# The gates of the final sum: made on all partitions by TensorE instead of loaded 128 times

## What is computed

```python
mod = (_silu(L0_c) @ L0_wmod).reshape(32, 6, 1, -1)
sa, ca, ga, sb, cb, gb = (mod[:, 0], ..., mod[:, 5])
gb = (2 * (gb >= 0) - 1) * jnp.maximum(jnp.abs(gb), 0.25)      # one row of 128 per sequence
...
x = x + gb * _L0_ffn_ref(h, ...)                               # x: (32, 256, 128)
```

## Time and profile before

| | us |
|---|---|
| three runs | 1588.82 (median), 1579.2, 2478.22 |
| profiled execution, its own time | 1589.78 |
| its span, first to last instruction | 1588.0 |
| of this, last stage (from SP's first row load) | 1536.1 to 1588.0 |
| busy: PE, DVE, ACT, POOL | 1366.6, 1180.9, 885.0, 868.0 |
| mean granted TensorE clock | 0.954 |

### The profile page before, as it was taken

The page is one execution under the profiler, slowest core; times in us unless marked ns, Lnnn a source line. Parts: engine busy times, 40 slices in busy tenths (PEclk is TensorE's granted clock), DMA queues, the critical chain, the costliest instruction groups (busy, mean ns, idle before and its releaser), DMA issues. The chain is left out here.

```text
span 1588.0 us, 42685 instructions
## 1 busy us (share of the span) xinstructions
PE 1366.6 (86%) x13344; PEld 1063.3 (67%) x13345; DVE 1180.9 (74%) x3082; ACT 885.0 (56%) x1918; POOL 868.0 (55%) x1279
## 2 busy tenths in 40 slices
PE   1499999999999999999999999962599999999950
PEld 1266777767777776777777676641588888888850
DVE  4567888888888888788888887866666666666647
ACT  1166777777777777777777777652133333333310
POOL 2045577677767767676776776663233333333334
PEclk9999999999999999999999999985799999999985
DMA  6433443444344354444434533300211111111139
GB/s 213 123 100 83 129 118 94 118 118 114 103 126 121 92 133 110 103 110 118 122 88 120 128 98 90 87 24 14 59 48 43 46 43 42 46 43 45 42 94 295
DMA packets 176591, 152.61 MB, mean 96 GB/s; under 512 B 21491, under 2 KB 159097, under 8 KB 176036
## 3 DMA queue, kind: packets, MB, share of 16 engines
q1 hardware_dynamic: 159096, 123.07, 30.1%
q0 software_dynamic: 8448, 16.93, 3.3%
q10 hardware_dynamic: 8880, 10.49, 1.9%
HBM read 89.37 MB, written 61.55 MB: 95 GB/s over the span
## 5 line engine op out<-in xcount | busy, mean ns | idle before, releaser
L988 ACT ACTIVATE probs<-p_exp 128x512 f32<-128x512 f32 x768 | 446.5, 603 | 183.6 <-PE p_exp L812 164.3
L1402 POOL TENSOR_SCALAR_AFFINE_SELECT probs<-probs 128x256 f32<-128x256 f32 (+1 forms) x768 | 365.4, 485 | 286.4 <-ACT probs L988 278.3
L1166 DVE TENSOR_REDUCE mx<-p_max 128x2 f32<-128x512 f32 x512 | 351.4, 687 | 169.9 <-PE p_max L786 168.9
L647 POOL DMA_INDIRECT pair_out<-on,v x136 | 133.6, 982 | 284.7 <-ACT on L557 279.3
L784 PE MATMUL p_max<-kt,qt 96*128 96x256 bf16 x1024 | 198.6, 275 | 40.5 <-DMA kt<-k_parts 19.7
L835 PE MATMUL p_out<-probs,v 128*32 128x256 f32 (+1 forms) x4096 | 221.0, 333 | 14.0 <-POOL probs L1402 7.5
L812 PE MATMUL p_exp<-qt,kt 100*128 100x256 bf16 x1024 | 196.7, 273 | 16.8 <-DMA qt<-max_parts 14.0
L621 DVE TENSOR_TENSOR ot<-ot,p_max 128x512 f32<-128x512 f32 x136 | 93.5, 688 | 125.8 <-PE p_max L508 106.5
L1169 DVE TENSOR_REDUCE mx<-p_max 128x4 f32<-128x512 f32 x256 | 173.2, 676 | 2.1 <-PE p_max L795 2.0
L835 PEld LDWEIGHTS p_out<-probs,v 128*32 128x32 f32 x4096 | 112.4, 109 | 85.4 <-POOL probs L1402 24.4
L1449 POOL DMA_INDIRECT rows_sorted<-h,idx x128 | 137.4, 1074 | 50.7 <-ACT probs L988 28.6
(11 more groups left out here) (169 smaller groups left out, 2757.9 us busy)
## 6 DMA issues: line engine op xcount, KB each, us to landing
qt<-q_parts SPq DMA_DIRECT2D x64, 384.0 KB
q_parts<-part_h SPq DMA_DIRECT2D x96, 128.0 KB, 2.0
kt<-k_parts SPq DMA_DIRECT2D x128, 96.0 KB
v<-rows_sorted SPq DMA_DIRECT2D x136, 65.0 KB, 1.8
q_parts<-part_m SPq DMA_DIRECT2D x64, 128.0 KB, 2.0
kt<-k_parts SPq DMA_DIRECT2D x128, 64.0 KB
qt<-pair_out SPq DMA_DIRECT2D x32, 256.0 KB, 5.4
mods<-mod_rows SPq DMA_DIRECT2D x32, 192.0 KB
```

The source lines that it names most:

```text
L647: nc.gpsimd.indirect_dma_start(pair_out, bass.IndirectOffsetOnAxis(rows_in[:, j.slot, DIM:DIM + 1].bitcast(U32), 0), rows_out[:, j.slot, : ...
L988: nc.scalar.activation(probs[:, g % 2, k, :], p_exp[:, k, :], ACT.Exp, scale=SCALE).then_inc(exp_done.sem, 1)
L1166: m = V.reduce_max(mx[:, w, 1, :, h8:h8 + 1].rearrange("p t o -> p (t o)"), p_max[:, bank, :].rearrange("p (t k) -> p t k", t=2), AX.X, ne ...
L1402: G.affine_select(out=blocks, in_=blocks, compare_op=ALU.is_ge, fill=zero, base=0, pattern=[[0, 2 if k < 2 else 4], [1, P]], channel_multi ...
```

## The change

The gate loads go. PE makes each group's gates on all partitions: a column of the identity, repeated 128 times as the stationary operand, times the 32 gate rows gives one sequence's row on every partition, so two matmuls fill 256 columns of a bank. Four banks serve as the four slots: the two of `p_exp` and the two of `p_max` whose expert products are over (PE waits for `hid_ready`). Before it fills a slot again, PE waits for the multiply four groups earlier (`fin_step`). DVE's multiply reads its gates from PSUM and waits for `gb_ps`, which PE raises once a group.

```diff
-        fin_gb = (pair_view[:, FIN_RING * NF:FIN_RING * (NF + GROUP * DIM)]
-                  .rearrange("p (a b c) -> p a b c", a=FIN_RING, b=GROUP))
+        fin_gb = (p_exp[:, 0, :], p_exp[:, 1, :], p_max[:, 0, :], p_max[:, 1, :])
...
-                sp.dma_start(fin_gb[:, g.slot, :, :],
-                             mod_rows[bass.ds(g.n * GROUP, GROUP), 3 * DIM:4 * DIM].unsqueeze(0)
-                             .to_broadcast([P, GROUP, DIM])).then_inc(fin_loaded[g.slot], 16)
...
             tiles(pe, body)
 
+            pe.wait_ge(hid_ready, FFN_TILES)
+            for g in range(NB // GROUP):
+                if g >= FIN_RING:
+                    pe.wait_ge(fin_step, 2 * (g - FIN_RING) + 2)
+                for j in range(GROUP):
+                    b = g * GROUP + j
+                    m = nc.tensor.matmul(fin_gb[g % FIN_RING][:, j * DIM:(j + 1) * DIM],
+                                         idf[0:NB, b:b + 1].to_broadcast([NB, P]), mrow[:, 3, :], start=True, stop=True)
+                m.then_inc(gb_ps, 1)
...
-                dve.wait_ge(fin_loaded[g.slot], 48 * (g.turn + 1))
+                dve.wait_ge(fin_loaded[g.slot], 32 * (g.turn + 1))
...
                 dve.wait_ge(fin_step, 2 * g.n + 1)
+                dve.wait_ge(gb_ps, g.n + 1)
                 fo = fin_out[:, g.slot, :].rearrange("p (b t c) -> p b t c", b=GROUP, c=DIM)
-                V.tensor_tensor(fo, fo, fin_gb[:, g.slot, :, :].unsqueeze(2).to_broadcast([P, GROUP, NT, DIM]), ALU.mult).then_inc(fin_step, 1)
+                gb = fin_gb[g.slot][:, 0:GROUP * DIM].rearrange("p (b c) -> p b c", b=GROUP)
+                V.tensor_tensor(fo, fo, gb.unsqueeze(2).to_broadcast([P, GROUP, NT, DIM]), ALU.mult).then_inc(fin_step, 1)
```

More of the change, by code:

```diff
@@ L313, in adaln_block @@
         fin_step = sem("fin_step")
+        gb_ps = sem("gb_ps")
         fin_done = sem("fin_done")
```

## The result

Over 20 runs each, the changed kernel takes 1578.97 us (median), the kernel before 1587.59 us (1588.82 in the three runs known ahead). The ratio is 0.9948, with an interval of 0.9933 to 0.9963: 5.9 to 10.6 us less, real, and well within 2%. One execution of each stands far outside (2478.22 us, and 2014.93 at a granted clock of 0.654) and is left out of the ratio. The forecast was 1582.6 us.

What follows compares the result with a forecast made beforehand. It took the last stage (52 us) to be paced mostly by DVE and POOL blocking each other. First POOL end 1542.65 + fifteen steps of 2.35 (35.25) + 2.96 + 1.78 gave 1582.6 us; range 1573 to 1590.

Steps and rivals of the forecast that it cites:

- Where the time lies: Only the last stage is at stake, from 1536.1 to 1588.0 us: 52 us or 3.3% of the span.
- The start: Last stage's first add waits for the second row load, not the gate load: gain 2.0 us, bounds 0 to 2.2.
- The new step: Time per group in the last stage, set between engines, DMAs and ring of four slots: 2.35 us.
- the late circle: DVE's add comes after POOL's start and waits for it, as before: 2.71 + 0.08 = 2.79 us a group.
- The mixture's share: Last stage: even mixture of groups with DVE's add after POOL's start (2.79) and before it (1.81): 2.30 us.
- The engines' lower bound: Last stage, DVE's add going before POOL's: port time alone is left, 0.55 + 1.26 = 1.81 us a group.
- The port-bound rival: Last stage: DMAs no limit, nearly every add first, steps of 1.81 to 1.95 us, 1574.5 to 1576.6 us; chance 0.2.
- The second wait: DVE's multiply in looped groups waits in a register instruction behind the add: 0.08 us more, bounds 0 and 0.15.
- The multiply: DVE's multiply, reading PSUM and SBUF, still takes 0.69 us and should not stand still for POOL.
- PE: PE's 32 added fp32 matmuls in the last stage: at most 1.9 us a group, made ahead, cost nothing.
- What bounded the kernel before: Last stage: circle of POOL's add, DVE's add, multiply and POOL's start, 2.71 us; gate load 0.85 us early.
- The sum: First POOL end 1542.65, fifteen steps 35.25, then 2.96 to the end: span 1580.9; with 1.78 more, 1582.6 us.

Runs made afterwards that it cites:

- e1: Changed kernel, but SP still loads every group's gates to SBUF, where nobody reads them: ratio 1.0006 to the kernel before, stage 52.0 us, step 2.83 us.
- e5: Changed kernel with the 16 groups of the last stage written out instead of a hardware loop: stage 44.8 us, step 2.35 us.
- e2: Changed kernel, but ACT copies the gates to SBUF and DVE's multiply reads them there: ratio 0.9945 to the kernel before, stage 44.8 us, step 2.36 us.
- e12: Kernel before the change, gate loads included, with the 16 groups of the last stage written out: stage 52.1 us, step 2.72 us.
- e3: Changed kernel without POOL's add of the residual: step 2.27 us.
- e8: Changed kernel with eight slots instead of four, groups written out, and without POOL's add of the residual: stage 41.6 us, step 2.23 us.
- e10: Changed kernel with eight slots, groups written out, row loads in 1 KB pieces: ratio 0.9928 to the kernel before, stage 41.1 us, step 2.13 us.
- e11: Changed kernel with eight slots, groups written out, row loads in 1 KB pieces, without POOL's residual add: stage 39.2 us, step 2.09 us.
- e4: Changed kernel with only the first of each group's two row loads: step 2.10 us on the whole, 1.67 us in runs of four groups.

## Why the prediction was right, point by point

- *Where the time lies* (the last stage alone, at most 52 us): right. Nothing outside it moved beyond scatter.
- *The start*: predicted 3.8 us from SP's first load to the first add, measured 3.94, before 5.81. A gain of 1.9 for the 2.0 forecast, and e1 shows that it comes from the wait, not the bytes: 3.91 with the gates' bytes still loaded.
- *The new step*: 2.35 forecast, 2.36 measured. The middle of three limits was taken, and the runs give each of them its size: DMAs 2.33 at 337 GB/s (forecast 2.32 by the old rate), engines alone 1.67 (forecast 1.81), the late circle 2.79 (forecast 2.79, seen in the changed kernel and in e1). The order turned round in part of the groups, as described.
- *The mixture's share*, partly luck: 2.30 was half the adds ahead of POOL at 1.81 and half behind at 2.79. It was one in three. Two late groups at 2.79 leave 1.54 of the 7.12 us for the third, so the mixture is 2.37; with the forecast's own 1.81 a third would have given 2.46. Two errors, of share and of price, nearly cancel.
- *The engines' lower bound* was mis-sized: 0.55 + 1.26 counts POOL's add as if it started when the port came free. Standing ready it needs 1.11 us. The port-bound rival would have been faster than I gave; it lost by the DMAs, as its counter-argument said: it needed over 403 GB/s, and 337 were to be had.
- *The second wait*: 0.08 us forecast, 0.12 to 0.14 us of gap instead of 0.03 measured. It lengthens the late circle (2.79 instead of 2.71), but without it (e5) the step is 2.35 instead of 2.36, since the row loads take its place.
- *The multiply*: 0.69 us and free of POOL, right, but e2 shows that this freedom is worth nothing here.
- *PE*: nobody waits, right; 1.22 us a group, bound 1.9. That the bound held is luck: it takes one row of line 539 for a matmul, but an fp32 matmul shows as two (1088 rows for 136 tiles of four matmuls), so worked out as it was it should have been 3.7. The four rows of a group take 0.31 us each, not 0.93.
- *What bounded the kernel before*: here the reading was too sure. I took the sum of 2.71 us "without any DMA in it" for proof that the gate load wasn't what set the pace, with 0.85 us to spare. Shown by e12: take 0.1 us out of the circle and the DMAs hold it at the same pace. The 333 GB/s of the earlier trace rows were within 1.2% of all that the DMAs give with such pieces. The forecast survived since its step was set between the limits instead of by the circle alone.
- *The sum*: predicted stage 44.8 us, measured 45.1. The forecast of 1582.6 is 3.6 us above the median, of which 2.2 are the profiled execution's distance from the kernel before's later median (1589.78 against 1587.59); the other 1.4 are within the interval of the ratio.

The Trainium skill ("DMA: Bandwidth & Descriptors", Where 436 GB/s comes from) gives about 358 GB/s as one core's limit. The windows have 337 GB/s in e3 and e8, where the DMAs hold the pace with pieces of 512 B, and 370 in e10 and e11, with row loads in pieces of 1 KB. One lies below it and one above; the measurement decides, and the page's figure is a guide but no ceiling. With pieces of 512 B the 2.20 us that it would give for the step were not within reach. By the same skill ("SBUF — State Buffer", Who interferes with whom) a DVE instruction with two SBUF inputs and a GpSimd (POOL) instruction that reads SBUF block each other, the later until the first is through. The traces agree in both orders: adds of 1.76 us behind POOL, POOL's of 1.53 to 1.55 us behind adds.

## What to carry to other kernels

When a sum of engine times closes exactly on the period, that shows one limit, not that there is no second one at the same place; before counting on the slack of a transfer, compare the rate of the stage with the best rate that the DMAs reach (here 333 with 337 GB/s), and read it from a window in the middle of the stage, not from the bytes of a step. A load that repeats a small row on all partitions costs its full bytes (2.69 or 2.83 us a group with them, 2.36 without); making it on an idle engine pays when the stage runs at the DMAs' rate, and the wait it removes is the smaller part. In this pipeline of a DVE add with two SBUF operands, a multiply and a POOL add, the order in which the two adds come decides the round (2.27 us with DVE's first in e2, 2.71 to 2.79 with POOL's first), so small shifts of arrival are worth more, or less, than their length.

## What was not expected of the hardware

- A blocked instruction that has been started ends sooner after its release than it takes alone: POOL's add 1.11 instead of 1.26 us, DVE's 0.55 instead of 0.69. A round with the add free and the multiply and POOL's add blocked is then 2.27 us (e2), and 1.67 where the multiply reads its gates from PSUM and isn't blocked (e4).
- Row loads in pieces of 1 KB instead of 512 B, with the same bytes, raised the DMA-bound rate from 337 to 370 GB/s in the settled part. Eight slots instead of four did not raise it (337 in both).
- The end of attention comes at times up to 12.3 us apart (1109.55 to 1121.88) in fourteen profiles of kernels with the same attention code, more than the whole effect of this change; from there to the last stage the time repeats within 1.8 us. What makes it scatter was not looked into.
